# A graph attention and feed-forward network on one core: joint factors for two norms in the last layer, and two graphs' sums moved ahead of a maximum in all layers

## What is computed

```python
x = _layernorm(x + _L0_gnn_ref(x, adj, ...), axis=-1)
# three layers, l = 0, 1, 2
si = x @ attn_w[l, :d]
sj = x @ attn_w[l, d:]
scores = si[:, :, None] + sj[:, None, :] + attn_b[l]
scores = jnp.where(scores >= 0, scores, 0.2 * scores)
scores = jnp.where(mask, scores, -jnp.inf)
attn = jax.nn.softmax(scores, axis=-1)
agg = jnp.einsum('bij,bjd->bid', attn, x)
h = layernorm(x + agg, g1[l], beta1[l])
ff = jax.nn.gelu(h @ W1[l] + b1[l], approximate=False) @ W2[l] + b2[l]
x = layernorm(h + ff, g2[l], beta2[l])
# after the layers
x = _layernorm(x0 + x, axis=-1)
```

## Time and profile before

| what | value |
|---|---|
| median of 3 runs | 1720.91 us (1720.08 to 1721.85) |
| the profiled execution | 1720.4 us |
| its span in the profile | 1718.6 us |
| granted TensorE clock, mean | 0.98 of full speed |
| busy PE / DVE / ACT / POOL | 1607.4 / 1347.8 / 1226.2 / 1335.0 us |
| busy GpSimd in the last 428 us | 382.9 us, where 420 us of the second layer have 321.5 |

### The profile page before, as it was taken

The page is one execution under the profiler, slowest core; times in us unless marked ns, Lnnn a source line. Parts: engine busy times, 40 slices in busy tenths (PEclk is TensorE's granted clock), DMA queues, the critical chain, the costliest instruction groups (busy, mean ns, idle before and its releaser), DMA issues.

```text
span 1718.6 us, 40460 instructions
## 1 busy us (share of the span) xinstructions
PE 1607.4 (94%) x11904; PEld 1424.9 (83%) x11904; DVE 1347.8 (78%) x5298; ACT 1226.2 (71%) x2852; POOL 1335.0 (78%) x2389
## 2 busy tenths in 40 slices
PE   4999999983999999999899999999999999999994
PEld 3888888872899899899788998998988888888894
DVE  1889889896877877877878778778787887888862
ACT  1888888883677777777667777777776777777763
POOL 5688888863578778778687787787778999999996
PEclk8999999996999999999999999999999999999997
DMA  6132233332122112112122221121211223222211
GB/s 199 63 100 90 94 98 98 95 104 66 50 74 98 58 52 73 55 54 73 37 74 74 84 73 45 65 73 39 71 62 38 74 73 97 74 73 76 71 50 49
DMA packets 145980, 127.48 MB, mean 74 GB/s; under 512 B 16513, under 2 KB 136833, under 8 KB 145921
## 3 DMA queue, kind: packets, MB, share of 16 engines
q1 hardware_dynamic: 138880, 124.30, 22.6%
q10 hardware_dynamic: 7040, 2.51, 0.7%
HBM read 89.04 MB, written 37.75 MB: 74 GB/s over the span
## 4 chain that ended last, share of the span: by engine, by line
PE 52%; POOL 16%; DVE 5%; issue 2%; ACT 1%; POOLq 0%; DVEq 0%; ACTq 0%
PE ps L45 22%; PE ps L897 22%; PE ps L870 3%; POOL xo L810 2%; POOL gnn_n L160 2%; POOL gnn_norm L804 2%; PE ps L884 2%; POOL gnn_norm L160 2%; POOL gnn_fin L823 2%; DVE gnn_junk L1022 2%; POOL inv L155 2%; PE ps L862 1%; POOL gnn_hb L793 1%; POOL gnn_hb L789 1%; PE ps L877 1%
## 5 line engine op out<-in xcount | busy, mean ns | idle before, releaser
L897 PE MATMUL ps<-gnn_w_hi,gnn_g_hi 128*128 128x256 f32 x1536 | 434.2, 283 | 0.0
L897 PE MATMUL ps<-gnn_w_lo,gnn_g_hi 128*128 128x256 f32 x1536 | 429.0, 279 | 0.0
L897 PE MATMUL ps<-gnn_w_hi,gnn_g_lo 128*128 128x256 f32 x1536 | 428.7, 279 | 0.0
L992 ACT ACTIVATE gnn_g_hi<-ps,b_cols 128x512 fp32r<-128x512 f32 x384 | 264.6, 689 | 205.9 <-PE ps L45 205.7
L45 PE MATMUL ps<-gnn_hT_hi,gnn_w_hi 128*128 128x512 f32 x768 | 339.1, 442 | 4.1 <-DVE gnn_g_lo L1093 4.1
L1093 DVE TENSOR_TENSOR gnn_g_lo<-ps,gnn_g_hi 128x512 fp32r<-128x512 f32 x384 | 262.7, 684 | 96.0 <-ACT ps L993 95.5
L45 PE MATMUL ps<-gnn_hT_hi,gnn_w_lo 128*128 128x512 f32 x768 | 304.0, 396 | 0.0
L45 PE MATMUL ps<-gnn_hT_lo,gnn_w_hi 128*128 128x512 f32 x768 | 303.8, 396 | 0.0
L897 PEld LDWEIGHTS ps<-gnn_w_lo,gnn_g_hi 128*128 128x128 f32 x1536 | 288.9, 188 | 2.2
L897 PEld LDWEIGHTS ps<-gnn_w_hi,gnn_g_hi 128*128 128x128 f32 x1536 | 288.8, 188 | 2.2
L897 PEld LDWEIGHTS ps<-gnn_w_hi,gnn_g_lo 128*128 128x128 f32 x1536 | 288.7, 188 | 0.0
(11 more groups left out here) (127 smaller groups left out, 3967.4 us busy)
## 6 DMA issues: line engine op xcount, KB each, us to landing
hist<-xo SPq DMA_DIRECT2D x48, 512.0 KB, 3.8
x<-hist SPq DMA_DIRECT2D x48, 512.0 KB, 3.9
aw<-in_L_gnn_attn_w SPq DMA_DIRECT2D x48, 256.0 KB, 4.1
gmask<-mask_hist SPq DMA_DIRECT2D x48, 256.0 KB, 4.1
att_xT_raw<-in_xT SPq DMA_DIRECT2D x16, 512.0 KB, 3.4
att_xl<-in_x SPq DMA_DIRECT2D x16, 512.0 KB, 3.6
gnn_fin<-hist SPq DMA_DIRECT2D x16, 512.0 KB, 3.9
out<-gnn_fin SPq DMA_DIRECT2D x16, 512.0 KB, 3.0
```

The lines of the kernel that those rows point to most:

```text
L897: mm = e.matmul(FF2[j % 2], g[a][:, m, j * N:(j + 1) * N], V[b][:, m, :], start=(n == 0), stop=(n == len(terms) - 1))
L992: e.activation(g[0][:, m, :], FF1[FFB[m]], ACT.Gelu, bias=bias)
```

## The change

The change has four parts.

In all layers, VectorE does the sums of graphs 0 and 1 of t+3 right behind residual 2 of graph 0, ahead of `probs_max`; the sum of graph 2 goes ahead of residual 2 of graph 2; only that of graph 3 stays behind `hT_lo`. In the last step of a layer both residues of W1 stand ahead of residual 2 of graph 2, and the sums of graphs 2 and 3 behind `hT_lo`.

In the last layer, `final_statistics` moves from behind residual 2 of graph 0 to behind `hT_lo`.

On GpSimd, the final sum of block t-1 moves behind n1 of t+1, ahead of hb.

The factors of the second norm of t and of the final norm of t-1 come from one chain of 128x8 operations (`both_norms`), since the statistics `mv3` now lie beside `mv2` in one tile. `last_factors` is left for the very last block.

```diff
+                def both_norms(t, par0, reused):
+                    n = t - 1 - FIRST
+                    rstd, shift3 = affine3[par0][:, 0, :], affine3[par0][:, 1, :]
+                    e.wait_ge(mv3_out, n + 1)
+                    e.tensor_tensor(inv3[:, 0, :], mv2[:, :, 1], eps[:], ALU.add).then_inc(ln2, 1)
+                    e.tensor_scalar(inv3[:, 1, :], mv2[:, :, 0], -1.0, None, ALU.mult).then_inc(ln2, 1)
+                    if reused:
+                        e.wait_ge(fin_out, START + n - 1)
+                    e.wait_ge(ln2, 5 * t + 1)
+                    e.tensor_tensor(rstd, inv3[:, 0, :], half_neg[:], ALU.pow).then_inc(ln2, 1)
+                    e.wait_ge(ln2, 5 * t + 3)
+                    e.tensor_tensor(shift3, inv3[:, 1, :], rstd, ALU.mult).then_inc(ln2, 1)
+                    hold_pool(e, ln2, 5 * t + 4).then_inc(norm3_out, 1)
...
                     if more >= 1:
-                        t1, p1, _ = ahead(q, par, 1)
-                        ln_attention(t1, p1)
+                        ln_attention(t1)
                     if final >= 2:
-                        t1, p1, _ = ahead(q, par, -1)
-                        final_factors(t1, p1, final == 3)
+                        final_sum(t0, p0, h0)
+                    if more >= 1:
+                        residual_rows(t1, p1)
...
                     residual2(t, par, 0)
-                    if final >= 2:
-                        final_statistics(q, par)
+                    if more >= 3:
+                        attention_sums(t3, p3, h3, 0)
+                        attention_sums(t3, p3, h3, 1)
                     if more >= 2:
                         probs_max(t2)
                     residual2(t, par, 1)
                     if layer_end:
                         split_w1_lo(layer_of(t1), 0)
-                    if more >= 3:
-                        attention_sums(t3, p3, h3, 0)
-                        attention_sums(t3, p3, h3, 1)
+                        split_w1_lo(layer_of(t1), 1)
+                    elif more >= 3:
+                        attention_sums(t3, p3, h3, 2)
                     residual2(t, par, 2)
-                    if layer_end:
-                        split_w1_lo(layer_of(t1), 1)
                     if more >= 1:
                         hT_lo(t1)
+                    if final >= 2:
+                        final_statistics(q, par)
+                    if layer_end:
+                        attention_sums(t3, p3, h3, 2)
                     if more >= 3:
-                        attention_sums(t3, p3, h3, 2)
                         attention_sums(t3, p3, h3, 3)
```

More of the change, by code:

```diff
@@ L146, in hold_pool @@
             n = holds["pool"] = holds["pool"] + 1
-            e.tensor_tensor(fence_pool[:, n:n + 1], half_neg[:, 0:1], half_neg[:, 0:1], ALU.add)
+            return e.tensor_tensor(fence_pool[:, n:n + 1], half_neg[:, 0:1], half_neg[:, 0:1], ALU.add)
         def layernorm_on_pool(e, chain, n0, stats, inv, y, dest, done=None):
-            e.tensor_tensor(inv[:, 0, :], stats[:, :, 1], eps[:], ALU.add).then_inc(chain, 1)
+            e.tensor_tensor(inv[:, 0, :], stats[:, :, 1], eps[:, 0:GROUP], ALU.add).then_inc(chain, 1)
             e.tensor_scalar(inv[:, 1, :], stats[:, :, 0], -1.0, None, ALU.mult).then_inc(chain, 1)
             e.wait_ge(chain, n0 + 1)
-            e.tensor_tensor(inv[:, 2, :], inv[:, 0, :], half_neg[:], ALU.pow).then_inc(chain, 1)
+            e.tensor_tensor(inv[:, 2, :], inv[:, 0, :], half_neg[:, 0:GROUP], ALU.pow).then_inc(chain, 1)
             e.wait_ge(chain, n0 + 3)
@@ L637, in gnn_kernel @@
             mv1 = sb("mv1", [P, GROUP, 2])
-            mv2 = sb("mv2", [P, GROUP, 2])
+            mv2 = sb("mv2", [P, 2 * GROUP, 2])
             fin = [sb(f"fin{i}", [P, GROUP, D]) for i in range(2)]
             st3 = sb("st3", [P, GROUP, 6])
-            mv3 = sb("mv3", [P, GROUP, 2])
-            inv3 = sb("inv3", [P, 2, GROUP])
-            affine3 = [sb(f"affine3_{i}", [P, 2, GROUP]) for i in range(2)]
+            mv3 = mv2[:, GROUP:2 * GROUP]
+            inv3 = sb("inv3", [P, 2, 2 * GROUP])
+            affine3 = [sb(f"affine3_{i}", [P, 2, 2 * GROUP]) for i in range(2)]
             fin_ld = sems("fin_ld_even", "fin_ld_odd")
@@ L795, in ln_attention, with ln_ffn @@
                     e.wait_ge(hb_out, t1 + 1)
-                def ln_ffn(t, par, half, last_layer):
+                def both_norms(t, par0, reused):
[11 more added lines that the diff above has]
+                    hold_pool(e, ln2, 5 * t + 4).then_inc(norm3_out, 1)
+                    for j in range(GROUP):
+                        ins = e.tensor_scalar(norm[:, j, :], y2[:, j, :], rstd[:, j:j + 1], shift3[:, j:j + 1],
+                                              ALU.mult, ALU.add)
+                    ins.then_inc(norm2_out, 1)
+                def ln_ffn(t, par, half, final):
                     l = layer_of(t)
+                    last_layer = final >= 1
                     e.wait_ge(mv2_out, t + 1)
-                    layernorm_on_pool(e, ln2, 5 * t, mv2, inv, y2, norm, norm2_out)
+                    if final >= 2:
+                        both_norms(t, 1 - par, final == 3)
+                    else:
+                        layernorm_on_pool(e, ln2, 5 * t, mv2[:, 0:GROUP], inv, y2, norm, norm2_out)
                     e.wait_ge(norm2_out, START + t + 1)
@@ L824, in final_sum, with last_factors @@
                     ins.then_inc(fin_sum, 1)
[L826 to L837, removed]
+                def last_factors():
+                    rstd, shift3 = affine3[1][:, 0, GROUP:2 * GROUP], affine3[1][:, 1, GROUP:2 * GROUP]
+                    e.wait_ge(mv3_out, NG)
+                    e.tensor_tensor(inv3[:, 0, 0:GROUP], mv3[:, :, 1], eps[:, 0:GROUP], ALU.add).then_inc(ln3, 1)
+                    e.tensor_scalar(inv3[:, 1, 0:GROUP], mv3[:, :, 0], -1.0, None, ALU.mult).then_inc(ln3, 1)
+                    e.wait_ge(fin_out, START + NG - 2)
+                    e.wait_ge(ln3, 1)
+                    e.tensor_tensor(rstd, inv3[:, 0, 0:GROUP], half_neg[:, 0:GROUP], ALU.pow).then_inc(ln3, 1)
+                    e.wait_ge(ln3, 3)
+                    e.tensor_tensor(shift3, inv3[:, 1, 0:GROUP], rstd, ALU.mult).then_inc(norm3_out, 1)
@@ L839, in body @@
                 def body(q, par, more, layer_end, final):
+                    t1, p1, _ = ahead(q, par, 1)
+                    t0, p0, h0 = ahead(q, par, -1)
                     if more >= 1:
[L841 to L842 removed]
+                        ln_attention(t1)
                     if final >= 2:
[L844 to L845 removed]
+                        final_sum(t0, p0, h0)
@@ L846, in body @@
+                    if more >= 1:
+                        residual_rows(t1, p1)
                     if layer_end:
                         split_w2_lo(layer_of(2 * q + par + 1))
[L848 to L852, removed]
+                    ln_ffn(2 * q + par, par, q, final)
+                ln_attention(0)
+                residual_rows(0, 0)
                 split_w2_lo(0)
```

16 lines of the change are left out of this document (10 added, 6 removed).

## The result

The changed kernel takes **1724.17 us** (median of 20 runs, 1721.41 to 1726.36); the kernel before, measured beside it in 20 runs, 1720.89. The ratio is 1.002, with a 95% interval of 1.0013 to 1.0027: 3.3 us slower, by the interval 2.2 to 4.6. I had forecast 1717.2, so 3.7 us faster. The time lies inside the range (1705 to 1725), the sign is wrong. The profiled execution took 1723.93 us with a span of 1722.1; before it was 1718.6.

The account below looks back on a forecast made before the run. TensorE's work (25.90 us a step) was taken to bound the first two layers, the loop through n1 the last. Terms -10.4 - 0.1 + 0.3 - 4.5 - 0.9 + 11.0 + 0.9 = -3.7 gave 1717.2 us, range 1705 to 1725.

Parts of the forecast that it names:

- What bounds the kernel: TensorE's own work, 25.90 us a step, in the first two layers; the loop through GpSimd's n1, 26.72, in the last.
- the odd steps: First two layers: four sums beside hb delay the maximum, TensorE waits 0.61 us in 16 odd steps, 9.8 us lost.
- Even steps: First two layers: the first sum gets through alone before hb, so only 0.05 us lost in each of 14 steps, 0.7.
- the forecast's slower rival: First two layers: sums meet hb from the first one in even steps too, 0.52 us wait each; 1724.9 us, chance 0.12.
- Layer ends: Steps ending the first two layers: h's residue no longer late but for 0.1 us, 4.5 us gained over two ends.
- The last layer: The loop through n1 shrinks to 25.6 us, below TensorE's 25.90, so TensorE bounds; 10.4 us gained over 12 steps.
- a sign of being wrong: The prediction called itself wrong if last-layer steps stayed above 26.4 us, or the first layers stayed at 25.90.
- the second rival: Last layer keeps part of its wait, through a slower 128x8 power and late VectorE; 3 to 4 us, 1720.5, chance 0.15.
- 0.9 us at the starts of the layers that never came: At two new layers' starts n1 waits less for sums, 0.45 us gained each.
- The step behind the second layer's end: Start of the last layer: n1 waits less for sums, 0.45 us gained.
- the tail: Program's end: final statistics ahead of the last residual 0.4 us too long, power 0.4, shape 0.1; 0.9 us lost.
- the first step's 0.5: The very first step also has hb early, so 0.5 us lost, within the first two layers' 11.0.

Follow-up runs that it names:

- Experiments 1 to 3: Changed kernel with old VectorE order in the first two layers' usual steps, 1710.92 us; changed kernel with hb held until the maximum, 1713.18; kernel before with that new order alone, 1731.08.
- Experiment 4: Kernel before with the new VectorE order only in the two steps that end a layer; 1716.27 us, ratio 0.9978.
- Experiment 5: Changed kernel with graph 3's sum moved ahead of residual 2 in the last layer; 1721.47 us, ratio 0.9998 to the kernel before.
- The first profile: Profile of the changed kernel from its main measurement, 1724.17 us; the second is from a rerun of the unaltered changed kernel, 1725.98 us.
- kernel 6: Changed kernel with old VectorE order in the first two layers' usual steps and graph 3's sum ahead of residual 2 in the last layer; 1707.2 us, ratio 0.9912.
- two small edits more: On the changed kernel: old VectorE order in the first two layers' usual steps, and the last layer's graph 3 sum ahead of residual 2; 1707.2 us.

## Why the prediction failed, point by point

**What bounds the kernel, and the odd steps: right.** hb starts at T - 3.70 where I had T - 3.76 (T being the unstalled 956.19), the sums take 3.45 where I had 3.36, and the transposes start at T + 0.61 as forecast. That this agrees to the last digit is luck: the sums take 0.09 more, and TensorE starts 0.05 us behind VectorE's maximum (956.80 against 956.75), where I had taken 0.13 from its start behind GpSimd's n1. Experiments 1 to 3 show this cause, from three sides. By the step clock a stalled odd step costs 0.68 on average. Odd and even steps together: +10.37 against 9.24 in the forecast for the same 28 steps.

**Even steps: right in mechanism.** The first sum is through alone, as I had it, and a step loses 0 to 0.2, on average 0.11 where I had 0.05. That the forecast's slower rival gave 1724.9, near the measured time, is chance: its mechanism, even steps that stall by 0.52, is refuted by the step clock.

**Layer ends: right.** -3.18 against -3.3. Experiment 4 adds that the order there takes the full 4.7 off these two steps when it stands alone.

**The last layer: the step that failed.** I put the loop at 25.6 us and so below TensorE's 25.9; it is 26.48 in one parity and 26.33 in the other, on the two sides of the 26.4 that I had named as a sign of being wrong. By the same pieces: T to the joint chain 10.04 (I had 9.9); chain to the end of xo, 1443.81 to 1454.43, 10.62 (10.4, as the 128x8 power takes 0.63 more than the 128x4 one, and I had taken 0.4); the step change 0.57 (0.5); n1's chain and n1, 1455.00 to 1460.11, 5.11 (4.8, since n1 takes 3.11 where it took 2.86 before); and 0.14 from n1's end to TensorE's first transpose, which I left out altogether, though I had used it elsewhere in the same text. Together 0.88 us. No single piece is off by more than 0.31; all five are off to the same side, and the distance to the bound was 0.3. The gain of a loop that passes below another bound is cut off on one side only: a loop shorter than forecast would have given nothing more, a longer one cost 12 times its excess. Here the twelve steps average 0.41 us over 25.90, 4.9 us, of which I had allowed 0.3: 4.6 us missed. Experiment 5 takes 1.7 us out of this loop, and 10.2 of the 10.4 us are there. I had priced this case as the second rival, with "3 to 4" us less and 0.15, although its two conditions were just the two uncertain terms; it deserved more than that. With the 4.6 us in it the sum is +0.9, near no change. That the kernel came out 3.3 us slower takes more, in the main 1.1 us more in the usual steps, and 0.9 us at the starts of the layers that never came.

**The step behind the second layer's end: wrong, but not through the change.** I had -0.45. The first profile has +1.60 with a clock at half level, the second +0.10 (28.95 against 28.85 before) and its own loss at the first end. The earlier sums brought nothing that shows to a layer's start: +0.10 at the second end where the clock stayed up, -0.12 at the first, where it falls before and after the change. The 0.9 us that I had for the two is in no profile (32.2 to 33.5 and 28.9 to 31.5 us, against 32.33 and 28.85). Why not stays open.

**Start and end of the program.** +0.80 for the tail against 0.9. The -0.29 of the ledger's first row hides the first step's 0.5. The stage's first copy comes 0.46 us earlier (407.75 against 408.21), ahead of anything that was changed. And the step itself takes 27.44 us against 27.23, at a granted clock that is low at its start and averages 0.96 after and 0.95 before; length times clock, an estimate, gives 26.3 against 25.9. Its stall is there, and the kernel before has none in this place:

```profile
451.38 1.09 PE L911 MATMUL ps<-ident,gnn_n 128*128 128x128 f32 x8 [0.32 <-DVE gnn_e L1083]
```

**Left open**: why n1 takes 3.05 to 3.11 us now and 2.86 before. It runs beside VectorE in both; in the first two layers' steps, ahead of hb, the same instruction takes 2.18 to 2.19. With the order of kernel 6 it takes 2.86 and 3.02 in turns. Which VectorE instruction costs it the rest wasn't tried.

## What to carry to other kernels

Work that is moved into an idle gap also leaves the place where it was, and the engine behind that place starts earlier: look at what then runs beside the moved work, because its own duration is only the lower bound. When a loop is forecast to fall just below another bound, add every handover to it, and set its margin against the sum of its uncertain terms, since errors there count on one side only and once per step. Where an edit has several parts, it pays to run each alone: here the parts were worth about +11, -4 and -5 us, and two small edits more turned 3.3 us lost into 14.5 us saved.

## What the hardware showed

- **Two engines in the same memory.** One sum instruction on VectorE takes 0.345 us alone and 0.86 from start to start (3.45 / 4) beside GpSimd's two-operand multiply; that multiply takes 0.705 (2.82 / 4) alone and 0.84 (3.37 / 4) beside the sums. Per pair both get through in about 0.86 us, less than 0.345 + 0.705 = 1.05. The Trainium skill's page "SBUF — State Buffer", section "SBUF: two separate sides", has the one that starts first keep the shared port pair for its whole instruction while the other blocks; the traces agree that the two exclude each other in good part, and not that the full time is lost. The shorter instruction, VectorE's, pays 0.52 us, the longer one 0.14.
- **A power on GpSimd** takes mostly 1.04 us for 128x4 and 1.67 for 128x8, where an add of either size takes 0.20. A straight line through the two sizes, an estimate, has 0.16 us per column and 0.4 that doesn't depend on them.
- **Handover to TensorE.** Its transposes start 0.05 to 0.06 us behind the end of the VectorE maximum that they wait for, and 0.14 to 0.16 behind the end of GpSimd's n1.
- **TensorE's clock** fell to its lower level in two of eleven profiles at the second layer's end, after a wait of 1.93 us that in another profile of the same kernel had no such effect, and waits of 2.45 and 2.46 us in two other kernels had none either. A single profile's step is therefore no measure of a change near such a wait; it moved a step here by 1.5 us.
